# Clipping the Y planes of bilinear hats in ScalarE's integer output instead of on VectorE

## The chip, the core and the metric

The program runs on one NeuronCore of a Trainium2 chip. The metric is the device time of one execution in microseconds. Three runs of the kernel before took 1015.71, 1015.75 and 1016.1 us; the median is 1015.75 us.

## What is computed

For 64 images the reference runs one transformer layer on tokens that a deformable convolution makes. A 4x4 patch convolution with batch norm and leaky ReLU gives a picture h of 96 channels and 21x21 pixels. A second convolution gives, for each of 25 output positions and 16 taps, an offset (dy, dx). The deformable convolution samples h bilinearly at the shifted points and multiplies by its weights; 77 text tokens are appended; quantised attention with an integer softmax and a feed-forward network follow. The sampling is what the change touches:

```python
y0 = jnp.floor(py); x0 = jnp.floor(px)
wy = py - y0; wx = px - x0
sampled = (v00 * (1 - wy) * (1 - wx) + v01 * (1 - wy) * wx
           + v10 * wy * (1 - wx) + v11 * wy * wx)      # 0 outside the picture
out = einsum('bckhw,ock->bohw', sampled, w) + b
```

A pixel (Y, X) has the weight max(0, 1 - |py - Y|) * max(0, 1 - |px - X|) in the sample at (py, px). Such a factor is called a hat.

## The kernel before

**Tiling.** For each image the 21x21 pixels are laid over the partitions in NCH = 4 chunks of ROWS = 6 picture rows (CH = 126 pixels). The free dimension is the SMP = 400 samples (16 taps x 25 positions). TensorE forms px - X (one plane, since each chunk holds the same columns) and py - Y for the first chunk in two PSUM banks (`hats` of the tensor block, lines 1179 and 1181). ScalarE takes the absolute value of the x plane (L644) and four times that of the y plane, each time with another constant added for the chunk's rows (L648), and writes five planes of 400 into one of four buffers HATS. VectorE makes min(|d| - 1, 0) of all five planes in one instruction (`hats`, stage HAT, L915) and multiplies the four Y planes by the x plane, broadcast (`weights`, stage HATW, L921); the two minus signs cancel. TensorE multiplies the products by the transposed picture (`interpolate`, stage INT, L1191 to L1195).

**Order.** Each engine runs its own list of stages, written out by hand in the string SLOT. An entry such as `dve.HAT.47` is an engine, a stage and a lag in images; `walk` runs the entries of each engine in that order for every group of four images. Nothing is reordered at run time: an instruction that waits holds all behind it on its engine. Around the change VectorE's list is (one group; the last number is the lag):

```
SUM.53 HAT.47 RCP.53 EXP.52 FF2.57 SUM.52 RCP.52 PR.54 FF2.56 HATW.47 PW.53 PR.53 PV3.55 RES.55
PW.52 PR.52 HAT.46 QKC.48 HATW.46 HAT.45 PV3.54 HATW.45 HAT.44 RES.54 LS2.55 PV3.53 LS2.54 RES.53 HATW.44
```

**Around it.** VectorE's other work is mostly the integer softmax: row sums (SUM, L1054), their reciprocals (RCP, L1059), after which GpSimd scales the rows (NRM, L563), ScalarE takes the logarithm (LOG, L740) and the ratio (PR on ScalarE, L747, into the single buffer RR), VectorE copies RR out (PW, L1069), which L747 of the next image waits for (`pw_done`), and makes powers of two (PR on VectorE, L1076); SyncE's queue then transposes them by DMA (L477). QKC (L968 to L972) casts queries and keys; SyncE's queue places the queries with 12 DMAs (L468), and TensorE's scores (L1276, L1279) wait for them. FF2 (L1096) adds the feed-forward result from PSUM to the residual, and PV3 and RES (L1082, L1089) do the same for attention. On ScalarE the rounding of queries and keys (L715, L717) frees the PSUM bank that TensorE's y matmul of the next hats (L1181) writes. The square (L734), the casts of V (L694), the normalised tokens (L686), the GELU (L761) and its table loads (L598) are the other ScalarE lines named below.

**Semaphores of the hats.** ScalarE raises `ax_done` once and `ay_done` four times an image; VectorE raises `hat_done` and `w_done`.

Of the kernel before, what the change touches and what calls it, by code (L numbers as in the profile page):

```python
# [32 lines left out]
SMP = TAPS * POS  # L33
# [4 lines left out]
CH = ROWS * HS  # L38
NCH = 4
LAST = NPIX - 3 * CH  # L40
HALF = CH // 2
SHIFT = 64 - HALF
# [14 lines left out]
MAGIC16 = 1536.0  # L57
RATIO_GAIN = 4.0 / 3.0 * (1.0 - 2.0 ** -9) * (1.0 + 1.0e-5) * 2.0 ** 112
BIG = 2.0 ** 111

# [122 lines left out]
def build(nc, x_col, txt, stem_w, stem_b, bn1, off_w, off_b, dcn_w, dcn_b, bn2, w_qkv, w_proj,  # L185
          b_proj, s_wqkv, s_wproj, s_act1, s_attn, s_act2, s_act3, w_in, b_in, w_out,
          c_lx, c_ly, c_base, c_mask, c_sum, c_later, c_ybias, c_ident, tok_scratch, out):
    dt, ALU, ACT = mybir.dt, mybir.AluOpType, mybir.ActivationFunctionType
    AX = mybir.AxisListType
    f32, bf16, f16, i8, i16, u16 = dt.float32, dt.bfloat16, dt.float16, dt.int8, dt.int16, dt.uint16  # L190
    with ExitStack() as ctx:
        def sb(name, shape, d=f32):
            return ctx.enter_context(nc.sbuf_tensor(f"{name}_sb", shape, d))

        def sem(name):
            return ctx.enter_context(nc.semaphore(name))

        bank = [ctx.enter_context(nc.psum_tensor(f"bank{b}", [128, 512], f32)) for b in range(6)]
# [44 lines left out]
        def col(k):  # L243
            return sc[:, k:k + 1]
# [13 lines left out]
        HATS = [sb(f"hats{i}", [SHIFT + CH, 1 + NCH, SMP]) for i in range(GRP)]  # L258
# [80 lines left out]
        ax_done, ay_done = sem("ax_done"), sem("ay_done")  # L339
# [8 lines left out]
        hat_done, w_done = sem("hat_done"), sem("w_done")  # L348
# [246 lines left out]
        def _(act):  # L595
# [42 lines left out]
            def hats(t):  # L638
                odd = t.i % 2
                rows = odd * SHIFT + CH  # L640
                if t.n >= GRP:
                    act.wait_ge(samp_full, t.count(1, 1 - GRP))
                act.wait_ge(dx_full, t.count(1, 1))
                nc.scalar.activation(HATS[t.i][0:rows, 0, :], bank[t.banks[0]][0:rows, 0:SMP], ACT.Abs).then_inc(ax_done, 1)  # L644
                act.wait_ge(dy_full, t.count(1, 1))
                for j in range(NCH):
                    line = ROWS * j - (ROWS // 2 if odd and j == NCH - 1 else 0)
                    nc.scalar.activation(HATS[t.i][0:rows, 1 + j, :], bank[t.banks[1]][0:rows, 0:SMP], ACT.Abs,  # L648
                                         bias=float(-line)).then_inc(ay_done, 1)

            def samples(t):
                act.wait_ge(samp_full, t.count(1, 1))
# [119 lines left out]
            def gelu_first_pair(t):  # L772

                if t.n == LAST_GROUP:
                    table(10)
                    for f in range(FT):
# [8 lines left out]
                       "XH1": lambda t: normalised(t, XA[:, t.i, :], SHIFT1, RSTD1, XH, rstd1_s, xt_full, xh_done),  # L785
                       "XH2": lambda t: normalised(t, X2[:, t.i, :], SHIFT2, RSTD2, XH2, rstd2_s, xt2_full, xh2_done, True),
                       "OFF": tap_quarters, "OFS": offsets, "STEM": stem, "HTT": pixels_first, "HAT": hats, "INT": samples, "DCN": dcn, "LN1X": xt1,
                       "LN2X": xt2, "V": v_round, "FFA": gelu_first_pair, **{f"FQ{k}": lambda t, k=k: qk_round(t, 2 * k) for k in range(2)}, "SC": scores, "SQ": square,
                       "LOG": log_probs, "PR": ratio, "PV2": o_round, "VC": v_cast, "OC": o_cast, **{f"FFN{f}": lambda t, f=f: gelu(t, 2 * f) for f in range(3)}})

        @block.vector
        def _(dve):
            step = [0]

            def then(ins):

                step[0] += 1
                ins.then_inc(prep, 1)
                dve.wait_ge(prep, step[0])

            v = nc.vector
# [7 lines left out]
            rows = bank[0][:, 0:3 * C1]  # L809
# [27 lines left out]
            def scalars():  # L837
# [32 lines left out]
                then(v.tensor_scalar(col(CC), col(CINT), 1.0, col(T0), ALU.max, ALU.subtract))  # L870
                then(v.tensor_scalar(col(OSC), col(CINT), 1.0, BIG, ALU.is_ge, ALU.mult))
                then(v.tensor_scalar(col(OSC), col(OSC), sc_in[:, 0:1], col(T2), ALU.mult, ALU.mult))
# [36 lines left out]
            sampling_constants()  # L909

            def hats(t):
                hat = HATS[t.i][0:t.i % 2 * SHIFT + CH, :, :]
                dve.wait_ge(ax_done, t.count(1, 1))
                dve.wait_ge(ay_done, t.count(NCH, NCH))
                v.tensor_scalar(hat, hat, -1.0, 0.0, ALU.add, ALU.min).then_inc(hat_done, 1)  # L915

            def weights(t):
                rows = t.i % 2 * SHIFT + CH
                hat = HATS[t.i][0:rows, :, :]
                dve.wait_ge(hat_done, t.count(1, 1))  # L920
                v.tensor_tensor(hat[:, 1:, :], hat[:, 1:, :], hat[:, 0:1, :].to_broadcast([rows, NCH, SMP]),  # L921
                                ALU.mult).then_inc(w_done, 1)
            def moments(t, st, mv, st_done, mv_done, xh_done, images=range(GRP)):

                dve.wait_ge(st_done, t.count(GRP, images.stop))
                if t.n >= 1:
                    dve.wait_ge(xh_done, t.count(GRP, 0))
                for i in images:
                    v.bn_aggr(mv[:, i, :], st[:, i, :]).then_inc(mv_done, 1)
# [174 lines left out]
            for k in range(3):  # L1104
# [3 lines left out]

            walk(dve, "dve", {
                "HAT": hats, "HATW": weights, **{f"PREP{k}": lambda t, f=f: f() if t.n < 1 else None  # L1110
                                                 for k, f in enumerate((fold_bn2, qkv_integers, qkv_weights, proj_weights))},
                "QKC": qk_cast, "MAX": row_min, "MXB": quarter_min, "MXC": last_min, "DST": distance,
# [297 lines left out]
```

## Time and profile before

| | |
|---|---|
| median of 3 runs | 1015.75 us |
| span of the profiled execution | 1014.5 us |
| TensorE (PE) matmuls busy | 880.8 us (87%) |
| VectorE (DVE) busy | 876.0 us (86%) |
| ScalarE (ACT) busy | 779.8 us (77%) |
| GpSimd (POOL) busy | 266.9 us (26%) |
| mean granted TensorE clock | 0.951 |
| VectorE's clip L915, 64 times | 76.5 us |
| VectorE's product L921, 64 times | 127.2 us |

Busy time is the time in which an engine had an instruction in its datapath; PEld is TensorE's loading of weights, which overlaps matmuls. In the rows below a time of a group of instructions stands before its mean in ns; idle time of an engine is put down to the instruction that ended it. "issue" is idle time for which the profile shows no releaser. Neighbouring instructions of one engine overlap by some tens of ns in the records, so the start of the next one is often the better measure. Durations of matmuls are modelled at their ends.

### The profile page before, as it was taken

How to read it: one execution, taken by the hardware profiler on the slowest of the kernel's cores; microseconds unless marked ns; L12 is line 12 of the kernel's file. 1: busy time of each engine (PE TensorE's matmuls, PEld its weight loads, DVE VectorE, ACT ScalarE, POOL GpSimd, SP SyncE). 2: the span in 40 equal slices, each digit the busy share in tenths (PEclk: the TensorE clock that was granted, in tenths of full speed). 3: DMA queues.
4: the chain of work that ended last, by engine and by line, in shares of the span. 5: the costliest groups of instructions: out<-in, count | busy, mean ns of one | idle time of the engine just before them, and what ended most of it. 6: DMA issues, size and time to landing. Idle time of an engine off the chain costs nothing. (4 is left out here: it accounts for less than half of the span.)

```text
span 1014.5 us, 18281 instructions
## 1 busy us (share of the span) xinstructions
PE 880.8 (87%) x5594; PEld 539.9 (53%) x5594; DVE 876.0 (86%) x1695; ACT 779.8 (77%) x1529; POOL 266.9 (26%) x248
## 2 busy tenths in 40 slices
PE   3568779999999999999999999999999999885757
PEld 1244436555565656565565656565556556453435
DVE  3964899998999899999999999999999999995960
ACT  2435587979888797979798988889797978785753
POOL 5210312315132313223041323141321414222120
PEclk9987769999999999999999999999999999998678
DMA  5110132221222232222213232323232232223030
GB/s 130 67 37 7 49 55 51 43 58 43 58 56 52 55 58 63 55 58 43 64 38 58 60 53 65 53 58 57 63 47 54 48 59 36 52 50 61 15 65 12
DMA packets 132628, 53.42 MB, mean 53 GB/s; under 512 B 105103, under 2 KB 131413, under 8 KB 132437
## 3 DMA queue, kind: packets, MB, share of 16 engines
q1 hardware_dynamic: 132532, 52.26, 24.5%
q8 instruction: 46, 0.75, 0.3%
q14 instruction: 50, 0.40, 0.1%
HBM read 19.75 MB, written 6.24 MB: 26 GB/s over the span
## 5 line engine op out<-in xcount | busy, mean ns | idle before, releaser
L563 POOL TENSOR_TENSOR ee_sb<-ee_sb,rs_sb 128x1020 f32<-128x1020 f32 x64 | 157.2, 2464 | 379.1 <-DVE rs_sb L1059 379.1
L1195 PE MATMUL bank<-hats_sb,ht_sb 127*96 127x400 f32 (+1 forms) x384 | 147.9, 522 | 1.7 <-DVE hats_sb L921 1.7
L1327 PE MATMUL bank<-w_out_sb,ge_sb 128*102 128x192 f32 x768 | 138.8, 331 | 10.9 <-DVE y_sb L1096 6.9
L1327 PEld LDWEIGHTS bank<-w_out_sb,ge_sb 128*102 128x102 f32 x768 | 120.3, 168 | 31.6 <-issue 17.8
L921 DVE TENSOR_TENSOR hats_sb<-hats_sb 126x1600 f32<-126x1600 f32 x64 | 127.2, 1987 | 0.7
L648 ACT ACTIVATE hats_sb<-bank 126x400 f32<-126x400 f32 (+1 forms) x256 | 108.2, 523 | 0.3 <-PE bank L1181 0.3
L727 ACT ACTIVATE a_sb<-scores,sc_sb 128x1020 f16<-128x1020 f32 x64 | 71.1, 1111 | 39.2 <-PE scores L1279 39.2
L1195 PEld LDWEIGHTS bank<-hats_sb,ht_sb 127*96 127x96 f32 (+1 forms) x384 | 58.7, 166 | 72.6 <-issue 69.3
L734 ACT ACTIVATE sq_sb<-rm_sb,sc_sb 128x1020 f32<-128x1020 f16 x64 | 73.5, 1148 | 18.2 <-DVE rm_sb L1031 18.0
L572 POOL TENSOR_TENSOR xshift_sb<-mv_sb,xshift_sb 102x4 f32<-102x4 f32 (+1 forms) x33 | 11.0, 333 | 279.9 <-DVE ve_sb L961 278.5
L1242 PE MATMUL bank<-xt_sb,w_in_sb 128*128 128x408 f32 (+1 forms) x204 | 82.0, 527 | 1.0 <-ACT xt_sb L667 1.0
L915 DVE TENSOR_SCALAR hats_sb<-hats_sb 126x2000 f32<-126x2000 f32 x64 | 76.5, 1195 | 5.9 <-ACT hats_sb L648 5.8
L1046 DVE SCALAR_TENSOR_TENSOR ee_sb<-sq_sb,sc_sb,ep_sb 128x1020 f32<-128x1020 f32 x64 | 79.9, 1249 | 0.1
L1054 DVE TENSOR_REDUCE ss_sb<-ee_sb 128x10 f32<-128x1020 f32 x64 | 77.4, 1209 | 2.1 <-DVE ee_sb L1046 0.5
L1003 DVE SCALAR_TENSOR_TENSOR m_sb<-a_sb,mx_sb 128x1020 f16<-128x1020 f16 x64 | 77.6, 1213 | 0.6
L1220 PE MATMUL bank<-ident_sb,xh_sb 102*128 102x102 f32 x256 | 51.4, 285 | 28.5 <-ACT xh_sb L686 18.3
L740 ACT ACTIVATE ee_sb<-ee_sb 128x1020 f32<-128x1020 f32 x64 | 68.9, 1077 | 9.3 <-POOL ee_sb L563 9.2
L747 ACT ACTIVATE rr_sb<-ee_sb 128x1020 uint16<-128x1020 f32 x64 | 68.6, 1072 | 2.6 <-DVE p_sb L1069 0.7
L1210 PE MATMUL bank<-wdcn_sb,samp_sb 128*100 128x192 f32 x384 | 69.4, 340 | 0.0
L1210 PEld LDWEIGHTS bank<-wdcn_sb,samp_sb 128*100 128x100 f32 x384 | 63.8, 173 | 4.7 <-issue 4.2
L761 ACT ACTIVATE ge_sb<-bank,b_in_sb 128x408 f32<-128x408 f32 (+1 forms) x102 | 51.8, 581 | 12.5 <-PE bank L1246 12.3
L1220 PEld LDWEIGHTS bank<-ident_sb,xh_sb 102*128 102x128 f32 x256 | 28.8, 149 | 58.8 <-ACT xh_sb L686 45.5
(168 smaller groups left out, 1862.7 us busy)
## 6 DMA issues: line engine op xcount, KB each, us to landing
xc_sb<-x_col SPq DMA_DIRECT2D x32, 165.4 KB, 3.2
out<-y_sb SPq DMA_DIRECT2D x32, 153.0 KB
xa_sb<-txt SPq DMA_DIRECT2D x16, 231.0 KB
xr_sb<-txt SPq DMA_DIRECT2D x16, 231.0 KB
q_sb<-qb_sb SPq DMA_DIRECT2D x192, 12.8 KB, 1.9
samp_sb<-samp_sb SPq DMA_DIRECT2D x48, 50.0 KB, 1.9
tok_scratch<-tokb_sb SPq DMA_DIRECT2D x16, 75.0 KB
xa_sb<-tok_scratch SPq DMA_DIRECT2D x16, 75.0 KB
```

The costliest lines, as they stand in the source:

```text
L563: nc.gpsimd.tensor_tensor(EE[b][:], EE[b][:], RS[b][:].unsqueeze(2).to_broadcast([128, RT, TOK]), ALU.mult).then_inc(scaled_done, 1)
L648: nc.scalar.activation(HATS[t.i][0:rows, 1 + j, :], bank[t.banks[1]][0:rows, 0:SMP], ACT.Abs, bias=float(-line)).then_inc(ay_done, 1)
L915: v.tensor_scalar(hat, hat, -1.0, 0.0, ALU.add, ALU.min).then_inc(hat_done, 1)
L921: v.tensor_tensor(hat[:, 1:, :], hat[:, 1:, :], hat[:, 0:1, :].to_broadcast([rows, NCH, SMP]), ALU.mult).then_inc(w_done, 1)
L1003: v.scalar_tensor_tensor(M16[b][:], A16[b][:], MAGIC16 + 128.0, MX[b][:].unsqueeze(2).to_broadcast([128, RT, TOK]), ALU.min, ALU.subtract) ...
L1046: v.scalar_tensor_tensor(EE[b][:].rearrange("p h k -> p (h k)"), SQ[:], sc[:, CC:CC + 1], EP[:].bitcast(bf16), ALU.add, ALU.mult).then_inc ...
L1054: v.tensor_reduce(SS[b][:], EE[b][:], AX.X, ALU.add).then_inc(ss_done, 1)
L1195: last = mm(dst, HT[0:rows, t.i, j, :], HATS[t.i][0:rows, 1 + j, :], start=(j == 0 and not odd), stop=(j == NCH - 2 and odd == 1))
L1210: last = mm(dst, SAMP[:, k, :, :].rearrange("c g p -> c (g p)"), WD[:, k, :], start=False, stop=(k == PACKED - 1))
L1220: last = nc.tensor.transpose(bank[t.banks[0]][:, c * TOK:(c + 1) * TOK], xh[b][:, 64 * c:64 * c + 128], ident[0:TOK, 0:TOK])
L1242: mm(bank[t.banks[first + c]][:, 0:n], weights(k + c, c), src[:, c, :], start=True, stop=False)
L1327: last = mm(bank[t.banks[0]][0:TOK, 0:D], GE[:, f, t.i * TOK:(t.i + 1) * TOK], WOUT[:, f, :], start=(f == 0), stop=(f == FT - 1))
```

## The change

Four edits. ScalarE's Y planes get the constant scale 2^31, an offset scaled likewise, and are written as 32-bit integers into the same buffer; the conversion is taken to saturate at 2^31, so that every |d| over 1 becomes 1. ScalarE's x plane gets the constant scale 2^-31. VectorE's clip works on the x plane alone (400 elements, not 2000), with -2^-31 in place of -1, and no longer waits for the Y planes. VectorE's product reads the Y planes as int32, adds -2^31 and multiplies by the x plane in one scalar_tensor_tensor, and it is the one that waits for the Y planes. Number and order of the instructions stay as they are on every engine.

```diff
+ONE_Y = 2.0 ** 31
@@ ScalarE, hats(t)
-                nc.scalar.activation(HATS[t.i][0:rows, 0, :], bank[t.banks[0]][0:rows, 0:SMP], ACT.Abs).then_inc(ax_done, 1)
+                nc.scalar.activation(HATS[t.i][0:rows, 0, :], bank[t.banks[0]][0:rows, 0:SMP], ACT.Abs,
+                                     scale=1.0 / ONE_Y).then_inc(ax_done, 1)
...
-                    nc.scalar.activation(HATS[t.i][0:rows, 1 + j, :], bank[t.banks[1]][0:rows, 0:SMP], ACT.Abs,
-                                         bias=float(-line)).then_inc(ay_done, 1)
+                    nc.scalar.activation(HATS[t.i][0:rows, 1 + j, :].bitcast(i32), bank[t.banks[1]][0:rows, 0:SMP], ACT.Abs,
+                                         scale=ONE_Y, bias=-line * ONE_Y).then_inc(ay_done, 1)
@@ VectorE
             def hats(t):
-                hat = HATS[t.i][0:t.i % 2 * SHIFT + CH, :, :]
+                hat = HATS[t.i][0:t.i % 2 * SHIFT + CH, 0, :]
                 dve.wait_ge(ax_done, t.count(1, 1))
-                dve.wait_ge(ay_done, t.count(NCH, NCH))
-                v.tensor_scalar(hat, hat, -1.0, 0.0, ALU.add, ALU.min).then_inc(hat_done, 1)
+                v.tensor_scalar(hat, hat, -1.0 / ONE_Y, 0.0, ALU.add, ALU.min).then_inc(hat_done, 1)
...
                 dve.wait_ge(hat_done, t.count(1, 1))
-                v.tensor_tensor(hat[:, 1:, :], hat[:, 1:, :], hat[:, 0:1, :].to_broadcast([rows, NCH, SMP]),
-                                ALU.mult).then_inc(w_done, 1)
+                dve.wait_ge(ay_done, t.count(NCH, NCH))
+                v.scalar_tensor_tensor(hat[:, 1:, :], hat[:, 1:, :].bitcast(i32), -ONE_Y,
+                                       hat[:, 0:1, :].to_broadcast([rows, NCH, SMP]), ALU.add, ALU.mult).then_inc(w_done, 1)
```

## Rows read from the trace of the kernel before

**Rows 1.** Busy time of each engine from 200 to 800 us, granted clock, DMA.
```profile
core 0: us, PE busy (x) PEld busy (x) DVE busy (x) ACT busy (x) POOL busy (x), PEclk, DMA share, GB/s
200.00:800.00 600.00, 568.43 (x3763) 350.45 (x3751) 567.30 (x1095) 516.86 (x1022) 167.01 (x152) 1.00 0.26 55
```

**Rows 2.** Waits from 200 to 800 us: us in total, times, longest.
```profile
DVE y_sb L1096 <- PE bank L1327: 10.2, 16, 1.0
...
PE bank L1220 <- ACT xh_sb L686: 8.4, 10, 0.9
...
PE scores L1276 <- issue: 3.3, 6, 1.0
PE bank L1181 <- ACT qk_sb L717: 2.4, 9, 0.3
...
ACT sq_sb L734 <- DVE rm_sb L1031: 10.6, 22, 0.6
```

**Rows 3.** Busy time in the two parts of one group, columns as in rows 1.
```profile
517.60:538.00 20.40, 18.26 (x119) 12.88 (x117) 18.58 (x33) 20.25 (x41) 5.42 (x4) 1.00 0.28 45
...
538.00:571.50 33.50, 33.35 (x229) 19.52 (x229) 32.59 (x68) 26.84 (x55) 8.91 (x9) 1.00 0.27 64
```

**Rows 4.** TensorE in order of time: start, duration, instruction, [idle before].
```profile
537.68 0.39 PE L1181 MATMUL bank<-rx_sb,ly_sb 9*126 9x400 bf16 x1 [0.28 <-ACT qk_sb L717]
```

**Rows 5.** ScalarE in order of time, same group.
```profile
531.26 0.38 ACT L694 ACTIVATE v_sb<-bank 102x192 int8<-102x192 f32 x1
531.47 1.11 ACT L740 ACTIVATE ee_sb<-ee_sb 128x1020 f32<-128x1020 f32 x1
...
534.52 0.40 ACT L694 ACTIVATE v_sb<-bank 102x192 int8<-102x192 f32 x1
535.04 1.06 ACT L747 ACTIVATE rr_sb<-ee_sb 128x1020 uint16<-128x1020 f32 x1
...
537.28 0.58 ACT L717 ACTIVATE qk_sb<-bank 128x204 int8<-128x204 f32 x2
```

**Rows 6.** VectorE in order of time, same group.
```profile
527.80 0.21 DVE L1059 RECIPROCAL rs_sb<-ss_sb 128x10 f32<-128x10 f32 x1
...
531.90 0.36 DVE L1096 TENSOR_TENSOR y_sb<-bank,x_sb 102x192 f32<-102x192 f32 x1 [0.72 <-PE bank L1327]
532.18 2.44 DVE L921 TENSOR_TENSOR hats_sb<-hats_sb 126x1600 f32<-126x1600 f32 x1
534.53 0.42 DVE L1069 TENSOR_SCALAR p_sb<-rr_sb 128x1020 bf16<-128x1020 uint16 x1
...
538.14 0.58 DVE L968 CAST qb_sb<-qk_sb 128x816 bf16<-128x816 int8 x1
```

**Rows 7.** L915 and L921 over the run: ns min/median/max, first and last start us.
```profile
L915 DVE TENSOR_SCALAR hats_sb<-hats_sb x64: 1190/1195/1203, 39.2 to 876.3; 126x2000 f32<-126x2000 f32 x32, 127x2000 f32<-127x2000 f32 x32
...
L921 DVE TENSOR_TENSOR hats_sb<-hats_sb x64: 1815/1826/3506, 40.4 to 878.8; 126x1600 f32<-126x1600 f32 x32, 127x1600 f32<-127x1600 f32 x32
```

**Rows 8.** VectorE in order of time: a clip-like instruction of 4 elements.
```profile
550.33 0.17 DVE L961 TENSOR_SCALAR ve_sb<-mv_sb 102x4 f32<-102x4 f32 x1
```

**Rows 9.** Groups of the page: count | busy us, mean ns | idle before, releaser.
```profile
L921 DVE TENSOR_TENSOR hats_sb<-hats_sb 126x1600 f32<-126x1600 f32 x64 | 127.2, 1987 | 0.7
L648 ACT ACTIVATE hats_sb<-bank 126x400 f32<-126x400 f32 (+1 forms) x256 | 108.2, 523 | 0.3 <-PE bank L1181 0.3
...
L915 DVE TENSOR_SCALAR hats_sb<-hats_sb 126x2000 f32<-126x2000 f32 x64 | 76.5, 1195 | 5.9 <-ACT hats_sb L648 5.8
L1046 DVE SCALAR_TENSOR_TENSOR ee_sb<-sq_sb,sc_sb,ep_sb 128x1020 f32<-128x1020 f32 x64 | 79.9, 1249 | 0.1
```

**Rows 10.** GpSimd in order of time.
```profile
528.09 4.84 POOL L563 TENSOR_TENSOR ee_sb<-ee_sb,rs_sb 128x1020 f32<-128x1020 f32 x2 [9.83 <-DVE rs_sb L1059]
```

**Rows 11.** SyncE's queue in order of time.
```profile
538.74 7.73 SPq L468 DMA_DIRECT2D q_sb<-qb_sb  x12
```

**Rows 12.** TensorE in order of time, at the start of the run.
```profile
42.29 4.21 PE L1195 MATMUL bank<-hats_sb,ht_sb 126*96 126x400 f32 x6 [1.70 <-DVE hats_sb L921]
```

**Rows 13.** A group of ScalarE, columns as in rows 9.
```profile
L686 ACT ACTIVATE xh_sb<-xa_sb,xshift_sb,rstd_sb 102x192 f32<-102x192 f32 x64 | 35.7, 558 | 1.0 <-POOL xshift_sb L575 1.0
```

More of the change, by code:

```diff
@@ L189, in build @@
     AX = mybir.AxisListType
-    f32, bf16, f16, i8, i16, u16 = dt.float32, dt.bfloat16, dt.float16, dt.int8, dt.int16, dt.uint16
+    f32, bf16, f16, i8, i16, u16, i32 = (
+            dt.float32, dt.bfloat16, dt.float16, dt.int8, dt.int16, dt.uint16, dt.int32)
     with ExitStack() as ctx:
```

## Prediction, made before the changed kernel was run

> **What bounds the kernel now.** I read four views, in this order. First the busy time of the engines in the steady stretch: between 200 and 800 us TensorE is busy 568.43 us of 600, VectorE 567.30, ScalarE 516.86, at full TensorE clock [rows 1]. Shares alone can't say which of the first two sets the pace: shortening one helps only where another engine waits for it. So, second, the waits of the same stretch [rows 2]. VectorE waits for TensorE at the final addition (L1096, 10.2 us in 16 places): it is ahead of TensorE there, a follower. TensorE waits for ScalarE: 8.4 us at the transposes of the normalised tokens (L1220), 2.4 us in 9 places at the y matmul of the hats (L1181), and 3.3 us in 6 places at the scores for something that isn't an instruction ("issue"); the code there waits for the queries, which SyncE's queue places. The one wait of a working engine for VectorE is ScalarE's at the square (10.6 us), and ScalarE waits for TensorE soon after.
>
> Third, one group of four images in order of time; a group takes some 55 us (the 16 groups' clips lie between 39.2 and 876.3 us [rows 7]; (876.3 - 39.2)/15 = 55.8 with the start). From the table load at 517.6 us to 538.0 us ScalarE is busy 20.25 of 20.40 us [rows 3], and TensorE, TensorE's next hats included, follows it: L1181 starts at 537.68 us after 0.28 us of waiting for ScalarE's L717 [rows 4]. From 538.0 to 571.5 us, where the next GELU begins, TensorE is busy 33.35 of 33.50 us [rows 3], ScalarE 26.84: ScalarE waits for TensorE there. The circle that sets the period is therefore some 20 us of ScalarE, then some 35 us of TensorE. VectorE matters only where it reaches into this circle.
>
> Fourth, I looked for such places below the threshold of the list of waits. There is one. ScalarE's cast L694 starts at 531.26 and the next instruction 0.21 us later; the same cast at 534.52 is followed only after 0.52 us, by L747 at 535.04 [rows 5]. L747 waits for VectorE to have read the previous ratios (pw_done); that is VectorE's L1069, 534.53 to 534.95. L1069 stands behind L921 of the first hats, which takes 2.44 us [rows 6] where the median product takes 1.826 [rows 7]. So about 0.3 us of the circle in each group is VectorE's.
>
> **The change part by part.** The span is 1014.5 us, the median 1015.75: 1.25 us lie around it, and the sum is made on the span.
>
> (1) VectorE's clip shrinks from 2000 to 400 elements. It takes 1195 ns now [rows 7, 9]. A line through the 4 elements of L961 (0.17 us [rows 8]) and the 2000 gives 0.17 + 396 x 0.5135 ns = 0.37 us. I take 0.82 us less each time, 64 x 0.82 = 52.5 us of VectorE's work, 3.3 us a group. Almost all of it lies beside TensorE or ScalarE work and is worth nothing by itself.
>
> (2) VectorE's product becomes a scalar_tensor_tensor with an int32 operand. Nothing in the trace reads int32. The nearest rows: the two-input fp32/bf16 L1046 at 1249 ns for 1020 elements, 1.225 ns each, against 1987/1600 = 1.242 ns for L921 [rows 9]. So the same, within 0.05 us; the bound above is 1600 x 1.225 = 1.96 us against some 1.83 without company, +0.13 us a product or 0.5 us a group, far under the 3.3 just freed.
>
> (3) ScalarE has the same 320 instructions; Y planes get a constant scale and write int32, the x plane a constant scale. L648 takes 523 ns now [rows 9]. L747 writes uint16, with a constant scale, in 1.06 us, and L740 writes as many f32 without one in 1.11 [rows 5]. I take 0, bounds -0.05 and +0.1 us each (the fourth rival).
>
> (4) The wait for the Y planes moves from the clip to the product. Behind the clip stand the reciprocal and the softmax of other images, which would now pass a late Y plane; but the Y planes are not late in the steady part: the clip waits for them today, 5.8 us in the whole run [rows 9], and the product comes later. Nothing.
>
> (5) What the freed 0.82 us triggers in front of ScalarE. The clip of the first hats stands just before the reciprocal (527.80) that starts GpSimd's two scalings: 528.09, 4.84 us, until 532.93 [rows 6, 10]. The product starts at 532.18, because the addition before it waits for TensorE (0.72 us [rows 6]); it overlaps GpSimd by 0.75 us and takes 0.61 us longer than alone. With the scalings 0.82 us earlier they end at 532.1, before the product begins; the product then takes 1.83 us, and L1069 ends at about 534.3. ScalarE's L747 can follow its cast at once (534.73): 0.3 us off the circle, and the 0.28 us that TensorE waits at L1181 go with it. The next limit is TensorE itself. How often: 64 products at 1.826 us would be 116.9 us, the group has 127.2 [rows 9]; 10.3 us over, or about 15 groups at 0.61 with one worse. I count 14 x 0.3 = 4.2 us.
> The Trainium skill (SBUF — State Buffer, § Who interferes with whom) says of VectorE with two SBUF inputs and GpSimd that whoever starts first holds the shared ports for the whole instruction. By that rule the product would be held until 532.93 and end at 534.7, where the row has 534.62; and it would make the new product, which also has two SBUF inputs, just as exposed, so that the gain hangs on the shift alone. With that shift missing the sum would be 4.2 us smaller.
>
> (6) The queries. VectorE's L968 starts at 538.14, right behind a clip, 0.28 us after ScalarE's L717 has ended (537.28 + 0.58) [rows 5, 6]. SyncE then issues 12 DMAs in 7.73 us [rows 11], and the scores wait for the last. With the clip short and L717 0.3 us earlier the queries leave about 0.45 us earlier, 0.15 more than TensorE gains. This counts only in the groups where the scores wait, 6 of 11 [rows 2]; say 8 in all, 8 x 0.15 = 1.2 us.
>
> (7) The start. The first clip (39.2 us [rows 7]) and product run one after the other, and TensorE's first interpolation waits for them until 42.29, for 1.70 us [rows 12]; tokens, and everything after, hang on this chain. 0.8 us.
>
> (8) The tail: the last clip starts at 876.3 us [rows 7], and the chain of waits there is softmax and feed-forward work. Nothing.
>
> Sum: 4.2 + 1.2 + 0.8 = 6.2 us. 1014.5 - 6.2 = 1008.3 us of span, 1009.6 us with the 1.25 around it. Bounds: if all 0.61 us of the product and 0.45 us of the queries counted in all 14 groups, 14.8 + 0.8 = 15.6 us, 1000 us; if the steady part gave only 0.1 us a group, 1.4 + 0.8, 1013.6 us.
>
> **The rivals.** Second: VectorE's time is covered everywhere. GpSimd may meet the product elsewhere, the SyncE queue may swallow the queries' lead, and TensorE may be just as late at L1181. Only the start remains: 1014.9 us. For it speaks that every term of the steady part is a few tenths.
>
> Third: VectorE is the bound after all, its 567.30 us level with TensorE's. Then the 3.3 us a group count until TensorE has no gap: it has 31.6 us of them in 600, 2.9 us a group, and 14 groups give up to 40 us, 976 us. Against it: TensorE's listed waits name ScalarE, and VectorE itself waits 10.2 us for TensorE. A part of it, some 1.5 us a group, would give 994 us.
>
> Fourth, the slower side: ScalarE pays for the constant scale or the int32 output in the hats. Ten of its twenty hat instructions of a group lie in the packed 20 us. Richer operands can cost: L686, with scale and bias from tensors, takes 558 ns for 192 elements, L694 0.38 us [rows 5, 13]; half of that difference is 0.09 us. At 0.09 each it is 10 x 0.09 = 0.9 us a group and 12.6 us in 14 groups, less the 6.2 gained: 1015.75 + 6.4 = 1022 us. It decides from 0.045 us each (10 x 14 x 0.045 = 6.3). Against it: constants stay constants, and L747 shows a constant scale without a price.
> The Trainium skill (ScalarE: Activation LUTs, § What ACT_TABLE_LOAD costs) gives about 93 ns for each operand that is read per partition and none for a constant; by that the price is nothing if the constants stay constants, and 93 ns otherwise.
>
> If the conversion did not saturate as meant, values would be wrong but no duration here depends on values.
>
> **How the numbers follow.** Forecast (1002 to 1013.7): 0.55. All covered (1013.7 to 1017.8): 0.20. VectorE the bound (under 1002): 0.10. ScalarE dearer or a new collision with GpSimd (over 1017.8): 0.15. A change of 0.2%, 2 us, is about what can be told from none. Faster 0.65, same 0.20, slower 0.15. The range 1002 to 1017.5 leaves out the third rival and most of the fourth.
>
> **What would show it.** Right: L915 near 0.37 us; the product of the first hats of a group near 1.83 instead of 2.44; L747 0.21 us behind the cast; TensorE's wait at L1181 gone; VectorE's busy time 50 to 60 us less, with more waiting for TensorE at L1096; TensorE's busy time unchanged. Wrong: a product well over 1.9 us, L648 over 0.55 us, products that meet GpSimd in other places, or a period that falls by more than 1 us, which would say that VectorE held TensorE up where no view shows it.

## The result and the profile after

The changed kernel takes 1024.62 us (median of 11 runs, 1016.94 to 1032.28); beside it on the same chip the kernel before took 1013.76 (11 runs, 1010.17 to 1016.1; the prediction's 1015.75 is the median of three of them). The ratio is 1.0101, interval 1.0076 to 1.0126: 1% slower, above the prediction's range of 1002 to 1017.5 us. One of the 11 runs, the 1032.28, was disturbed and is not in the ratio.

The profiled execution has a span of 1014.8 us, as long as the one of before with its 1014.5. It was the shortest of its 11 runs while the profiled run of before, at 1015.75, was near the longest of its own, so the two totals must not be compared; the groups inside must. First the page and its groups (columns as in rows 9; "busy us, mean ns | idle before"):

```profile
PE 876.3 (86%) x5594; PEld 537.0 (53%) x5594; DVE 844.4 (83%) x1695; ACT 780.7 (77%) x1529; POOL 247.9 (24%) x248
L1330 PE MATMUL bank<-w_out_sb,ge_sb 128*102 128x192 f32 x768 | 138.6, 330 | 22.6 <-DVE y_sb L1099 18.7
L924 DVE SCALAR_TENSOR_TENSOR hats_sb<-hats_sb 126x1600 f32<-126x1600 int32 x64 | 126.0, 1969 | 3.2 <-ACT hats_sb L651 2.6
L651 ACT ACTIVATE hats_sb<-bank 126x400 int32<-126x400 f32 (+1 forms) x256 | 108.2, 523 | 0.3 <-PE bank L1184 0.3
L1049 DVE SCALAR_TENSOR_TENSOR ee_sb<-sq_sb,sc_sb,ep_sb 128x1020 f32<-128x1020 f32 x64 | 100.4, 1569 | 1.5
```

Lines have moved by 2 or 3: L924 is the product, L651 ScalarE's Y planes, L1049 the exponential (before L1046), L1330 the second feed-forward product (before L1327), L917 the clip, L1062 the reciprocal, L565 GpSimd's scaling, L1099 the feed-forward addition (before L1096). ScalarE's hats cost what they cost in [rows 9], 523 ns; the product's mean is 1969 ns after 1987, its median 1825 after 1826 [rows 7]. The clip has shrunk as worked out. But one group that the change does not touch has grown: the exponential, from 79.9 us to 100.4 [rows 9], which takes back 20.5 of the 53 us that the clips give. GpSimd's 64 scalings have fallen by 12 us, from 157.2 to 145.6. Each instruction's range shows how:

```profile
L917 DVE TENSOR_SCALAR hats_sb<-hats_sb x64: 356/360/369, 38.6 to 876.6; 126x400 f32<-126x400 f32 x32, 127x400 f32<-127x400 f32 x32
L924 DVE SCALAR_TENSOR_TENSOR hats_sb<-hats_sb x64: 1812/1825/3508, 39.0 to 879.7; 126x1600 f32<-126x1600 int32 x32, 127x1600 f32<-127x1600 int32 x32
L1049 DVE SCALAR_TENSOR_TENSOR ee_sb<-sq_sb,sc_sb,ep_sb x64: 1217/1273/2931, 106.6 to 970.8; 128x1020 f32<-128x1020 f32 x64
```

The median exponential takes 1.27 us, but in most groups of four images one takes 2.93. Now the waits of TensorE from 200 to 800 us, after, which answer [rows 2]:

```profile
PE bank L1330 <- DVE y_sb L1099: 9.4, 10, 1.0
PE bank L1223 <- ACT xh_sb L689: 9.0, 11, 0.9
...
PE bank L1184 <- ACT qk_sb L720: 3.6, 8, 0.5
```

In the kernel before the first of these waits stood there once, for 0.6 us; now TensorE waits 1.02 to 1.03 us for VectorE's feed-forward addition in nine of the ten groups between 245 and 751 us (the tenth wait of the line is 0.2 us). The wait at the y matmul, which was to vanish, has gone from 2.4 us to 3.6. The group that [rows 4 to 6, 10] show, in order of time, first VectorE, then GpSimd, ScalarE and TensorE:

```profile
523.93 0.36 DVE L917 TENSOR_SCALAR hats_sb<-hats_sb 126x400 f32<-126x400 f32 x1
524.20 0.21 DVE L1062 RECIPROCAL rs_sb<-ss_sb 128x10 f32<-128x10 f32 x1
524.53 2.93 DVE L1049 SCALAR_TENSOR_TENSOR ee_sb<-sq_sb,sc_sb,ep_sb 128x1020 f32<-128x1020 f32 x1
527.38 0.34 DVE L1099 TENSOR_TENSOR y_sb<-bank,x_sb 102x192 f32<-102x192 f32 x1
...
528.88 0.22 DVE L1062 RECIPROCAL rs_sb<-ss_sb 128x10 f32<-128x10 f32 x1
...
530.35 2.46 DVE L924 SCALAR_TENSOR_TENSOR hats_sb<-hats_sb 126x1600 f32<-126x1600 int32 x1
532.74 0.41 DVE L1072 TENSOR_SCALAR p_sb<-rr_sb 128x1020 bf16<-128x1020 uint16 x1
...
524.49 1.89 POOL L565 TENSOR_TENSOR ee_sb<-ee_sb,rs_sb 128x1020 f32<-128x1020 f32 x1 [8.97 <-DVE rs_sb L1062]
529.18 1.95 POOL L565 TENSOR_TENSOR ee_sb<-ee_sb,rs_sb 128x1020 f32<-128x1020 f32 x1 [2.80 <-DVE rs_sb L1062]
...
523.34 1.17 ACT L737 ACTIVATE sq_sb<-rm_sb,sc_sb 128x1020 f32<-128x1020 f16 x1
533.24 1.05 ACT L750 ACTIVATE rr_sb<-ee_sb 128x1020 uint16<-128x1020 f32 x1 [0.46 <-DVE p_sb L1072]
...
527.88 2.17 PE L1330 MATMUL bank<-w_out_sb,ge_sb 128*102 128x192 f32 x12 [1.03 <-DVE y_sb L1099]
535.88 0.39 PE L1184 MATMUL bank<-rx_sb,ly_sb 9*126 9x400 bf16 x1 [0.46 <-ACT qk_sb L720]
```

And the same places in the kernel before, of which [rows 6] has the reciprocal (527.80); the last line is the first of the two scalings of [rows 10]:

```profile
526.69 1.20 DVE L915 TENSOR_SCALAR hats_sb<-hats_sb 126x2000 f32<-126x2000 f32 x1
...
527.92 1.22 DVE L1046 SCALAR_TENSOR_TENSOR ee_sb<-sq_sb,sc_sb,ep_sb 128x1020 f32<-128x1020 f32 x1
529.06 0.35 DVE L1096 TENSOR_TENSOR y_sb<-bank,x_sb 102x192 f32<-102x192 f32 x1
...
528.09 2.81 POOL L563 TENSOR_TENSOR ee_sb<-ee_sb,rs_sb 128x1020 f32<-128x1020 f32 x1 [9.83 <-DVE rs_sb L1059]
```

The reciprocal releases two things: GpSimd, which starts 0.29 us after it, and VectorE's own next instruction, the exponential. Before, the clip took 1.20 us ahead of the reciprocal; by then ScalarE's square, the exponential's input, had long been done, so the exponential followed the reciprocal within 0.12 us, 0.17 us ahead of GpSimd, and took 1.22 us. The two met before the change too, but GpSimd was the one that paid: 2.81 us for a scaling that takes 1.89 when it comes first. After, the reciprocal comes 0.84 us earlier and the square ends at 523.34 + 1.17 = 524.51. GpSimd starts at 524.49, the exponential at 524.53, 0.04 us behind it, and takes 2.93 us: 1.85 of them until GpSimd is through at 526.38, and 1.08 after that. The addition behind it is late, TensorE waits 1.03 us; the second reciprocal is late, so that GpSimd's second scaling (529.18 to 531.13) meets the product after all (2.46 us), ScalarE's L750 waits 0.46 us for L1072 and TensorE as long at the y matmul.

How often: the start of the second product of a group marks the period. From the third group to the last, before, it goes from 148.41 to 871.40 us in 13 groups, 55.61 us each; after, from 141.95 to 872.57, 56.20 each. The exponential takes 2.93 us in 12 of these 13 groups. The one group without shows how thin the margin is:

```profile
691.84 0.21 DVE L1062 RECIPROCAL rs_sb<-ss_sb 128x10 f32<-128x10 f32 x1
692.08 1.28 DVE L1049 SCALAR_TENSOR_TENSOR ee_sb<-sq_sb,sc_sb,ep_sb 128x1020 f32<-128x1020 f32 x1
...
696.83 1.99 DVE L924 SCALAR_TENSOR_TENSOR hats_sb<-hats_sb 126x1600 f32<-126x1600 int32 x1
...
692.13 5.01 POOL L565 TENSOR_TENSOR ee_sb<-ee_sb,rs_sb 128x1020 f32<-128x1020 f32 x2 [9.06 <-DVE rs_sb L1062]
```

Here the square ended at 692.05, the exponential started 0.05 us before GpSimd, and it took 1.28 us; the product took 1.99.

### The profile page after: what moved, and what is told of

The parts are those of the page before. It is cut to its first block and busy times, and to the rows that moved or that the text cites. A ratio compares the mean times of both kernels' runs of the same rounds, so it can differ in the third digit from the quotient of the medians.

```text
span 1014.8 us, 18282 instructions
## 1 busy us (share of the span) xinstructions
PE 876.3 (86%) x5594; PEld 537.0 (53%) x5594; DVE 844.4 (83%) x1695; ACT 780.7 (77%) x1529; POOL 247.9 (24%) x248
## 5 line engine op out<-in xcount | busy, mean ns | idle before, releaser
L565 POOL TENSOR_TENSOR ee_sb<-ee_sb,rs_sb 128x1020 f32<-128x1020 f32 x64 | 145.6, 2278 | 409.1 <-DVE rs_sb L1062 409.1
L1330 PE MATMUL bank<-w_out_sb,ge_sb 128*102 128x192 f32 x768 | 138.6, 330 | 22.6 <-DVE y_sb L1099 18.7
L1330 PEld LDWEIGHTS bank<-w_out_sb,ge_sb 128*102 128x102 f32 x768 | 120.3, 168 | 43.6 <-issue 29.8
L924 DVE SCALAR_TENSOR_TENSOR hats_sb<-hats_sb 126x1600 f32<-126x1600 int32 x64 | 126.0, 1969 | 3.2 <-ACT hats_sb L651 2.6
L651 ACT ACTIVATE hats_sb<-bank 126x400 int32<-126x400 f32 (+1 forms) x256 | 108.2, 523 | 0.3 <-PE bank L1184 0.3
L1049 DVE SCALAR_TENSOR_TENSOR ee_sb<-sq_sb,sc_sb,ep_sb 128x1020 f32<-128x1020 f32 x64 | 100.4, 1569 | 1.5
L750 ACT ACTIVATE rr_sb<-ee_sb 128x1020 uint16<-128x1020 f32 x64 | 67.7, 1058 | 6.2 <-DVE p_sb L1072 5.5
L1140 PE MATMUL bank<-xc_sb,stem_w_sb 49*96 49x441 f32 x128 | 45.0, 597 | 13.6 <-DMA xc_sb<-x_col 11.2
```

The source lines that it names most:

```text
L565: nc.gpsimd.tensor_tensor(EE[b][:], EE[b][:], RS[b][:].unsqueeze(2).to_broadcast([128, RT, TOK]), ALU.mult).then_inc(scaled_done, 1)
L651: nc.scalar.activation(HATS[t.i][0:rows, 1 + j, :].bitcast(i32), bank[t.banks[1]][0:rows, 0:SMP], ACT.Abs, scale=ONE_Y, bias=-line * ONE_Y ...
L924: v.scalar_tensor_tensor(hat[:, 1:, :], hat[:, 1:, :].bitcast(i32), -ONE_Y, hat[:, 0:1, :].to_broadcast([rows, NCH, SMP]), ALU.add, ALU.mu ...
L1049: v.scalar_tensor_tensor(EE[b][:].rearrange("p h k -> p (h k)"), SQ[:], sc[:, CC:CC + 1], EP[:].bitcast(bf16), ALU.add, ALU.mult).then_inc ...
L1330: last = mm(bank[t.banks[0]][0:TOK, 0:D], GE[:, f, t.i * TOK:(t.i + 1) * TOK], WOUT[:, f, :], start=(f == 0), stop=(f == FT - 1))
```

## The experiments

Theory A, formed from these two traces: the loss is the reversed order of GpSimd's scaling and the exponential, nothing else; without that reversal the change gains. "Collision" below means that the exponential is the one that waits. Theory B: the integer rows or the product that reads them cost the time. Each kernel was run beside the kernel before, whose median was 1013.75, 1012.6, 1010.67 and 1010.8 us in the four comparisons. "Period" below is the mean over the 13 groups, read as above.

**The changed kernel again.**

> The changed kernel itself beside the three others on one chip. Theory A and B: 1.008 to 1.013 times the kernel before, the exponential L1049 at 2.9 us in 12 of 13 steady groups. If the ratio lies under 1.003 here, the loss depends on the chip or the run and the group's period (56.2 us against 55.6) must differ from the first profile too.

1.0079 (1.0048 to 1.0111), 1019.68 us, period 56.09, exponential at 2.93 us in the same 12 groups. The loss is no accident of one comparison.

**The exponential ahead of the reciprocal, in the changed kernel.**

```diff
-pe.HTT.4 act.LOG.13 dve.RCP.53 act.LN1X.8 dve.EXP.52 pe.LN1X.11
+pe.HTT.4 act.LOG.13 dve.EXP.52 act.LN1X.8 dve.RCP.53 pe.LN1X.11
```

> The changed kernel with one swap in the order of VectorE: the exponential of the third image (entry dve.EXP.52, line L1049) is issued before the reciprocal of the fourth (dve.RCP.53) instead of behind it. Theory A (GpSimd's scaling, released by that reciprocal, gets the shared ports just ahead of the exponential in the changed kernel, which takes 2.93 us instead of 1.22 in 12 of 13 steady groups): the exponential takes 1.2 to 1.3 us in every group, PE's wait for the feed-forward addition before its product L1330 falls from 1.03 us per group to under 0.1, the group goes from 56.2 to about 55.0 us and the time to 1000 to 1011 us, below both kernels. Theory B (the loss lies in the 32-bit integer rows themselves: ScalarE, or the product that reads them): the exponential becomes short but the time stays within 0.3% of the changed kernel's, some 1.01 times the kernel before.

0.9972 (0.9942 to 1.0002), 1011.39 us (0.4 above the range in us, beside a kernel before of 1013.75), and in a second comparison:

> The changed kernel with the exponential of the third image ahead of the reciprocal of the fourth once more, for a narrower interval beside the others on this chip: theory A 0.994 to 0.999 times the kernel before (its first comparison gave 0.9972, interval 0.9942 to 1.0002). If it lies above 1.000, the swap only makes up the loss and the change gains nothing.

0.9958 (0.9934 to 0.9982), 1006.8 us against 1010.67. One swapped pair turns 0.8 to 1% slower into 0.3 to 0.4% faster; the interval of the second comparison lies below 1. VectorE and GpSimd at the place, first comparison's trace:

```profile
523.03 1.28 DVE L1049 SCALAR_TENSOR_TENSOR ee_sb<-sq_sb,sc_sb,ep_sb 128x1020 f32<-128x1020 f32 x1 [0.24 <-ACT sq_sb L737]
524.23 0.21 DVE L1062 RECIPROCAL rs_sb<-ss_sb 128x10 f32<-128x10 f32 x1
...
524.52 3.92 POOL L565 TENSOR_TENSOR ee_sb<-ee_sb,rs_sb 128x1020 f32<-128x1020 f32 x2 [10.36 <-DVE rs_sb L1062]
```

The exponential now waits for the square by itself (0.24 us) and GpSimd can't start under it. All 64 are short, and TensorE's wait at L1330 from 200 to 800 us is 0.2 us, in one place. Period 55.07 and 55.40 us.

**The same swap in the kernel before.**

> The kernel before with the same swap (exponential of the third image ahead of the reciprocal of the fourth), nothing else. Theory A: there the exponential already starts 0.17 us ahead of GpSimd's scaling and is short, so the swap can only delay the reciprocal, and with it the scaling, by up to 1.2 us: within 0.4% of the kernel before, 1012 to 1018 us. If it gains as much as the swap in the changed kernel does, the gain there is the swap's own and says nothing of the change.

1.0048 (1.0022 to 1.0074), 1017.26 us, period 55.96: slower, a bit more than I had said. The exponential was safe there already; the reciprocal now comes 1.2 us later, GpSimd with it, and the product of the first hats meets more of it (2.83 us in most groups, where the kernel before has 2.55 in most and 2.44 in the group of [rows 6]). So the swap gains only with the short clip, and the gain of the kernel above is not the swap's own.

**Only the clip, without integers.** The Y planes are not clipped here; that part of the computation is left out.

```diff
@@ kernel before, VectorE
-                hat = HATS[t.i][0:t.i % 2 * SHIFT + CH, :, :]
+                hat = HATS[t.i][0:t.i % 2 * SHIFT + CH, 0, :]
                 dve.wait_ge(ax_done, t.count(1, 1))
-                dve.wait_ge(ay_done, t.count(NCH, NCH))
@@ weights(t)
                 dve.wait_ge(hat_done, t.count(1, 1))
+                dve.wait_ge(ay_done, t.count(NCH, NCH))
```

> The kernel before with the clip on the x plane alone and the wait for the Y planes moved to the product; ScalarE writes float32 as before and the product is the plain two-tensor product. The Y planes are not clipped: that part of the computation is left out. Theory A (the time moves because 0.82 us of VectorE's work goes from ahead of the exponential): the same as the changed kernel, 1.006 to 1.013 times the kernel before, with the exponential at 2.9 us in most groups. Theory B (integer output or the product of three operands costs the time): 0.4 to 0.8% faster than the kernel before.

1.0059 (1.0026 to 1.0093), 1019.24 us, period 56.15, and the exponential of the changed kernel (from 200 to 800 us; busy, mean ns | idle before):

```profile
L1046 DVE SCALAR_TENSOR_TENSOR ee_sb<-sq_sb,sc_sb,ep_sb 128x1020 f32<-128x1020 f32 x42 | 67.8, 1615 | 1.1
```

The ratio is a hair below the 1.006 to 1.013 expected, but the loss is there without one integer row or one product of three operands, far from theory B's gain. Theory B falls. With the swap on top:

> The kernel before with the clip on the x plane alone (the Y planes are not clipped: that part of the computation is left out), float32 throughout, the plain two-tensor product, and the exponential of the third image issued before the reciprocal of the fourth. Theory A: the same as the changed kernel with that swap, 0.994 to 1.000 times the kernel before, exponential at 1.3 us. Theory B (the integer rows cost time by themselves): faster than the changed kernel with the swap by 0.3% or more.

0.9978 (0.9952 to 1.0004), 1008.28 us, period 55.10: within the noise the same as the integer version with the swap (0.9958 in the same comparison, 0.9934 to 0.9982), as theory A wanted, and not faster than it, as theory B did.

**VectorE's time given back at the one place.** A memset of a spare tile behind the clip of the first image of a group; 0.68 us in the trace.

```diff
                 v.tensor_scalar(hat, hat, -1.0 / ONE_Y, 0.0, ALU.add, ALU.min).then_inc(hat_done, 1)
+                if t.i == 0:
+                    v.memset(PAD[:, 0:750], 0.0)
```

> The changed kernel with 0.8 to 0.9 us put back on VectorE behind the clip of the first image of each group alone (a memset of a spare tile of 128x750 float32, one a group; 14 of the 52.5 us taken away are given back). It lies between the clip and the reciprocal that releases GpSimd. Theory A (only the reciprocal's place against the exponential's matters): the exponential L1049 is at 1.2 to 1.3 us again, PE's wait before L1330 is gone, and the time is within 0.3% of the kernel before or up to 0.6% faster (1006 to 1016 us), although VectorE has more to do than in the changed kernel. Theory B (the integer rows or their product cost the time): slower than the changed kernel or the same, 1.008 to 1.015 times the kernel before.

0.9979 (0.9946 to 1.0012), 1010.16 us, period 55.30; no exponential takes more than 1.28 us, and TensorE's wait at this addition is gone from 200 to 800 us. More work on VectorE, and the kernel is 1% faster than without it. The opposite, the memset behind the three other clips and not behind the first (`if t.i > 0`):

> The changed kernel with the same 0.8 to 0.9 us put back behind the clips of the second, third and fourth image of each group (42 of the 52.5 us), and nothing behind the first. Theory A: the exponential stays at 2.9 us in most groups and the time stays 0.4 to 1.3% above the kernel before; the time of the other three clips was covered and giving it back costs under 0.3%. Theory B: as slow as this too, so this kernel is to be read with the one before it: theory A wants this one slow and that one fast.

1.0102 (1.0054 to 1.015), 1021.76 us, period 56.53, with 13 long exponentials. Three quarters of the freed time given back cost nothing that can be told from the changed kernel (1.0101 and 1.0079); the quarter at the reciprocal decides alone.

**A fifth of the pad.** The same as the first of these with 150 elements.

> The changed kernel with a memset of 128x150 float32, an estimated 0.15 to 0.25 us (128x750 took 0.68 us), behind the clip of the first image of each group. In the changed kernel GpSimd's scaling starts at 524.49 us and the exponential, whose input is there at 524.51, at 524.53: 0.04 us late. Theory A (whoever starts first holds the ports for its whole instruction): 0.15 us is enough to turn the order round, the exponential is 1.2 to 1.3 us in most groups and the time is 0.995 to 1.002 times the kernel before, as with the pad of 0.68 us. Theory C (the loss grows evenly with how much earlier the scaling comes, and has no threshold): a fifth of the pad buys back about a fifth of the loss, 1.005 to 1.009.

0.9978 (0.9949 to 1.0008), 1010.0 us. VectorE and GpSimd at the place:

```profile
522.12 0.18 DVE L920 MEMSET pad_sb<- 128x150 f32 x1
522.22 0.15 DVE L1065 RECIPROCAL rs_sb<-ss_sb 128x10 f32<-128x10 f32 x1
522.39 1.28 DVE L1052 SCALAR_TENSOR_TENSOR ee_sb<-sq_sb,sc_sb,ep_sb 128x1020 f32<-128x1020 f32 x1
...
527.14 1.99 DVE L927 SCALAR_TENSOR_TENSOR hats_sb<-hats_sb 126x1600 f32<-126x1600 int32 x1
...
522.46 5.00 POOL L566 TENSOR_TENSOR ee_sb<-ee_sb,rs_sb 128x1020 f32<-128x1020 f32 x2 [8.94 <-DVE rs_sb L1065]
```

0.18 us a group buy back the whole 1%: the exponential starts 0.07 us before GpSimd, and every one of the 64 is short. A loss that grew evenly with the lead of the scaling (theory C) would have come back by a fifth only; it has a threshold. Over the 14 steady groups of this kernel the exponential leads GpSimd by 0.06 to 0.17 us and takes at most 1.28 us; in the changed kernel, where the two meet there, it is 0.04 or 0.05 us behind and takes 2.92 or 2.93, and 0.05 or more ahead and takes at most 1.28. Nothing lies between in these two kernels. One exponential of the kernel with the pad behind three clips does not fit the order of the records:

```profile
853.33 3.00 DVE L1052 SCALAR_TENSOR_TENSOR ee_sb<-sq_sb,sc_sb,ep_sb 128x1020 f32<-128x1020 f32 x1
853.37 1.89 POOL L566 TENSOR_TENSOR ee_sb<-ee_sb,rs_sb 128x1020 f32<-128x1020 f32 x1 [11.66 <-DVE rs_sb L1065]
```

By the records it starts 34 ns ahead of GpSimd, and is held all the same. So the starts in the trace tell who wins only down to some 0.04 us. Against the kernel with the small pad (period 55.24) the collision costs 56.20 - 55.24 = 0.96 us a group; TensorE's new wait, 1.03 us in 12 of 13 groups, makes 0.95 of it, but the two periods are not known that well (see step (7) below).

**The pad behind all four clips.**

> The changed kernel with 0.68 us put back on VectorE behind each of the four clips of a group: 32-bit integer rows, clip of the x plane alone and the product of three operands stay, only VectorE's time is nearly what it was. Theory A: 0.998 to 1.003 times the kernel before, with short exponentials. Theory B (the integer rows or the product of three operands cost time by themselves): 1.006 or more.

0.9994 (0.9968 to 1.0021), 1009.41 us, with no exponential over 1.28 us. With VectorE's time nearly what it was, the integer rows cost nothing that can be measured.

**The collision made in the kernel before.** No work is changed; the reciprocal is issued ahead of the clip.

```diff
-... dve.SUM.53 act.V.11 dve.HAT.47
-pe.HTT.4 act.LOG.13 dve.RCP.53 act.LN1X.8 dve.EXP.52 ...
+... dve.SUM.53 act.V.11 dve.RCP.53
+pe.HTT.4 act.LOG.13 dve.HAT.47 act.LN1X.8 dve.EXP.52 ...
```

> The kernel before with the clip of the fifth image (five planes, 1.20 us) issued behind the reciprocal that releases GpSimd's scaling instead of ahead of it, nothing else: the work of every engine is the same, only the scaling is released 1.1 to 1.2 us earlier against the exponential, as the change does by shortening the clip. Theory A: GpSimd holds the ports when the exponential comes; clip and exponential together take 3.7 to 4.3 us instead of 2.4, the feed-forward addition is late, PE waits before L1327 about 1 us a group, and the time is 1.005 to 1.015 times the kernel before, without any of the change in it. Theory D (the loss needs the changed kernel's integer rows or its shorter clips elsewhere): within 0.3% of the kernel before.

1.0298 (1.025 to 1.0345), 1042.76 us, period 57.65: the direction of theory A, which leaves nothing of theory D, but twice the top of its range and three times the loss of the changed kernel.

```profile
539.56 1.15 DVE L915 TENSOR_SCALAR hats_sb<-hats_sb 126x2000 f32<-126x2000 f32 x1
540.62 2.91 DVE L1046 SCALAR_TENSOR_TENSOR ee_sb<-sq_sb,sc_sb,ep_sb 128x1020 f32<-128x1020 f32 x1
...
539.72 2.74 POOL L563 TENSOR_TENSOR ee_sb<-ee_sb,rs_sb 128x1020 f32<-128x1020 f32 x1 [8.70 <-DVE rs_sb L1059]
...
PE bank L1327 <- DVE y_sb L1096: 18.4, 12, 1.7
```

GpSimd comes 0.16 us after the clip and is itself held: 2.74 us instead of the 1.89 above, 0.85 more. Once the clip is done it goes first, and the exponential, just behind, takes 2.91. Clip and exponential together take 4.06 us, inside the 3.7 to 4.3 expected; what was mis-sized is the consequence: TensorE waits 1.6 to 1.7 us in nearly every group (last line, waits from 200 to 800 us; its 12 waits fall into 10 groups), not 1: here no clip is shortened, so the addition is late by the whole of the collision. From the reciprocal, which started at 539.42, to the addition at 543.46 it is 4.04 us, where the kernel before has 2.37 from the clip to the addition, 1.67 less. The period grows by 2.0. A little of the rest is the clock: in six of these 13 groups the granted clock falls to 0.50 for 3.4 us, starting inside this wait or at most 0.8 us behind it, and in a seventh elsewhere, where the kernel before has one such stretch in all; over the groups at full clock the period grows by 1.9 (57.30 after 55.40). The last 0.2 stay open.

## Why the prediction was wrong

**What bounds the kernel.** Right: ScalarE and TensorE set the period and VectorE matters only where it reaches in. The third rival (VectorE's 3.3 us a group count) is refuted by the pad behind three clips, which changed nothing that can be told. But "There is one", of the places where it reaches in, was wrong. There was a second, the feed-forward addition, at which TensorE waited in one group of the kernel before for 0.6 us. I read in [rows 2] that VectorE waits for TensorE at this addition, and took VectorE to be ahead there; that wait belongs to the addition at 531.90. The one before it (529.06 us, directly behind the exponential) had no wait on either side, which tells nothing of its slack. Counted from the start of the clip it came after 2.37 us (529.06 - 526.69) and now comes after 3.45 (527.38 - 523.93): 1.08 us later, and TensorE waits 1.03 us. In the last experiment it is 1.67 us later and TensorE waits 1.60 in the same group. Its slack was under 0.1 us.

**Step (1)** held: 0.36 us against 0.37, 53.4 us for 52.5. VectorE's busy time fell by only 31.6 us, because the exponentials took 20.5 back (step (5)).

**Steps (2), (3), (4)** held: the product and ScalarE's Y planes as above. The fourth rival, which had my weight on the slower side, failed by its mechanism although the time came out near its 1022 us: ScalarE pays nothing.

**Step (5)** failed, at its first sentence. It says that the scalings come 0.82 us earlier, and follows that to the product, seven instructions on. It did not ask what else stands between: the exponential directly behind the same reciprocal, which also has two SBUF inputs and whose own input comes from ScalarE and did not move. GpSimd came forward by 0.84 us, the exponential could not follow. Both rows were at hand: in the trace of before the exponential leads GpSimd by 0.17 us, and a shift of 0.84 in one of them had to be held against it. [rows 10] said more: two scalings took 4.84 us there, where one takes 1.89 when it comes first; the exponential was already making GpSimd wait, and step (5) moved this sum forward as if it were the scalings' own. I even quoted the rule that decides it, in the Trainium skill (SBUF — State Buffer, § Who interferes with whom): whoever starts first has the shared ports for the whole instruction. The trace agrees with it (2.93 us with GpSimd 0.04 us ahead, 1.28 with it 0.05 behind); only the exponential above that led by 34 ns does not. But I applied it (with 532.93 + 1.83 = 534.76 rounded to 534.7) to one pair of instructions, not to every pair that the shift re-orders. The "new collision with GpSimd" stood in the chances as half of a line of 0.15, without a place or a price; that is the case that came.

The rest of step (5) shows once the cause is out of the way: in the kernel with the small pad the product of the first hats takes 1.99 us in 12 groups, where the kernel before has mostly 2.43 to 2.56, and TensorE's wait at the y matmul, 2.4 us in [rows 2], is no longer among its waits of that stretch. What that is worth the times don't tell. The kernel with the large pad keeps a product of 2.33 to 2.46 us and 1.9 us of that wait, and its ratio is the same, 0.9979 against 0.9978. Over the groups at full clock its period is 55.05 us against 54.76, 0.3 more, the size of step (5), from one trace each. And 2.4 us in 600 is some 3 us in 14 groups, less than the 4.2 that I put there.

**Step (6)** is not shown. In the kernel with the small pad the scores' wait is 1.5 us in 4 places instead of 3.3 in 6 [rows 2], but two profiled runs of the kernel with the swap have 1.3 in 3 and 2.6 in 7.

**Step (7), the start.** TensorE's first interpolation starts at 40.9 us instead of 42.29 [rows 12]. Its wait there is 0.59 to 0.85 us in the eight profiled runs with a short first clip and nothing or the small pad behind it, and 1.38 to 1.70 in the three with the old clip: the 0.8 us of this step. The total hardly shows it, because the start varies by more. The second product of the third group came at 141.95 instead of 148.41 in the profiled runs, but this isn't the change's: two profiled runs of one and the same kernel, the one with the swap, have it at 149.7 and 142.0. Busy time and clock from 20 to 40 us, first and second comparison (columns as in rows 1; the clock is the last number but two):

```profile
20.00:40.00 20.00, 5.27 (x13) 2.07 (x13) 15.79 (x38) 5.15 (x13) 6.43 (x5) 0.57 0.56 163
...
20.00:40.00 20.00, 5.39 (x14) 2.18 (x14) 16.40 (x38) 5.67 (x14) 6.44 (x5) 1.00 0.53 159
```

The run with the late start was granted 0.57 there; the one with the early start 1.00. The kernel before had 1.00 there too and still started late, so what decides the start is open. Over the 13 profiled runs of all these kernels the second product of the third group starts between 141.95 and 151.54 us, which is more than most of what is discussed here; hence the periods.

The periods vary as well: 55.07 and 55.40 us in these two runs of one kernel. The difference goes with the clock. Two neighbouring groups of the second run:

```profile
692.70:748.01 55.31, 52.43 (x350) 32.27 (x349) 49.73 (x102) 48.05 (x96) 13.57 (x14) 1.00 0.26 56
748.01:805.18 57.17, 54.01 (x350) 33.62 (x349) 49.63 (x102) 47.94 (x96) 15.70 (x14) 0.97 0.26 53
```

In the second one the granted clock is 0.50, the lower of TensorE's two levels, for 3.4 us from 768.54, behind a wait of TensorE of 0.76 us, and the group is 1.9 us longer. The first run has one such group among the 13, the second three, the kernel before and the changed kernel one each, the kernel with the small pad three. Over the other groups the two runs have 54.89 and 54.87 us, the kernel before 55.40, the changed kernel 56.00 and 55.93, the kernel with the small pad 54.76. So the order of the kernels stands, the collision costs 1.1 to 1.2 us a group by this count, and tenths of a microsecond in the plain periods say nothing.

**The sum.** With the collision gone the change is worth 0.2 to 0.4% (0.9978 with the small pad, 0.9972 and 0.9958 with the swap): 2 to 4 us of the 6.2 forecast, all of the right sign. The intervals of the first two reach 1. By the groups at full clock, with one trace of the kernel before, it is 0.5 to 0.6 us a group, where steps (5) and (6) had 0.4. The version to keep is the changed kernel with the exponential ahead of the reciprocal.

## What to carry to other kernels

When an instruction gets shorter, list everything that the instructions behind it release on other engines, and for each one ask which neighbours keep their old time because their input comes from elsewhere; every pair whose order flips is a candidate, and with a resource that is held for a whole instruction a flip by 0.04 us moves the whole wait from one engine to the other, here 1.65 us (2.93 against 1.28) onto VectorE in 12 of 13 groups. In the kernel before GpSimd bore it (2.81 instead of 1.89) and TensorE did not wait for it: an instruction that takes longer than its fellows is a sign of such a pair before anything flips. Issue the instruction that needs the shared resource before the one that releases its competitor, rather than trust a lead of tenths of a microsecond. And an addition or copy that nobody waits for in the trace has an unknown slack, not an endless one.

## What the runs showed of the hardware

A plain clip of 2000 fp32 elements with one SBUF input keeps GpSimd's two-input scaling waiting (2.74 us instead of 1.89 in the last experiment). The Trainium skill (SBUF — State Buffer, § Who interferes with whom) lists tensor_scalar among those that can take the shared pair, and that trace agrees. In the kernel before this clip ends at 527.89 us, ahead of GpSimd's 528.09, and plays no part. What I had not expected is the margin: 0.1 us in the end of ScalarE's square, within one program, divides the 12 groups with the collision from the one without. ScalarE's 32-bit integer output and VectorE's reading of it cost the same as float32, 523 ns for 400 elements and 1825 for 1600.
